# Bit-linear stage: the largest value of each token found hidden block by hidden block on TensorE, four blocks rounded on GpSimd, and the experts' semaphores cleared one stage later

## The reference, cut to what matters

```python
def act_quant(x):
    scale = 127.0 / jnp.clip(jnp.max(jnp.abs(x), axis=-1, keepdims=True), 1e-05)
    return jnp.clip(jnp.round(x * scale), -128, 127) / scale

def bit_linear(x, w):
    xq = x + jax.lax.stop_gradient(act_quant(x) - x)
    wq = w + jax.lax.stop_gradient(weight_quant(w) - w)
    return jnp.einsum('bsd,hd->bsh', xq, wq)

h = bit_linear(x, w1)                                    # 256 -> 1024
h = depthwise_conv1d(h.transpose(0, 2, 1), conv_w, conv_b)   # 3 taps along the tokens
h = h.transpose(0, 2, 1)
h = jax.nn.silu(h)
return bit_linear(h, w2)                                 # 1024 -> 256
```

## Time and profile before

| | us |
|---|---|
| median of 3 runs | 638.29 |
| lowest and highest | 637.61, 638.93 |
| the profiled execution, its own time | 635.03 |
| its span (first to last instruction) | 633.3 |

### The profile page before, as it was taken

How to read it: one execution, slowest core, us unless ns; L and a number is a source line. 1 busy time by engine, 2 the same in 40 slices (tenths; PEclk the granted TensorE clock), 3 DMA queues, 4 the chain that set the end, 5 groups by cost and what they waited for, 6 DMA issues and landing times. The chain is left out here.

```text
span 633.3 us, 14611 instructions
## 1 busy us (share of the span) xinstructions
PE 538.1 (85%) x5264; PEld 460.8 (73%) x5264; DVE 366.0 (58%) x1114; ACT 361.5 (57%) x859; POOL 194.2 (31%) x285
## 2 busy tenths in 40 slices
PE   3899999999977249999999996688999999977565
PEld 2777778888765149999999996667878888756344
DVE  3667666757664811131223103589778877866986
ACT  2678778878764003333222333378788787865544
POOL 2032535335314251111122002621333544424071
PEclk9989999999999559999999998899999999997778
DMA  6472012110201996766755523320201110000001
GB/s 164 141 201 80 27 50 75 52 50 8 73 2 31 331 374 193 278 178 210 258 167 173 166 79 87 110 85 9 93 2 51 51 51 2 3 2 1 1 0 59
DMA packets 33529, 62.79 MB, mean 99 GB/s; under 512 B 4162, under 2 KB 24467, under 8 KB 33332
## 3 DMA queue, kind: packets, MB, share of 16 engines
q1 hardware_dynamic: 29716, 47.97, 23.5%
q0 software_dynamic: 2928, 10.75, 5.8%
q10 hardware_dynamic: 816, 3.15, 1.3%
HBM read 51.11 MB, written 10.75 MB: 98 GB/s over the span
## 5 line engine op out<-in xcount | busy, mean ns | idle before, releaser
L1576 ACT ACTIVATE ex_h_t<-ex_h,b_e 128x128 f32<-128x128 f32 x168 | 48.0, 368 | 125.7 <-PE ex_h L1760 125.7
L1166 PEld LDWEIGHTS a_ring<-ident,w_all 112*125 112x125 f32 x768 | 88.7, 188 | 23.7 <-issue 12.7
L1166 PE MATMUL a_ring<-ident,w_all 112*125 112x112 f32 x768 | 100.1, 280 | 6.4 <-ACT w_all L626 6.3
L634 ACT ACTIVATE w_all<-a_ring 125x448 f32<-125x448 f32 x128 | 62.8, 542 | 45.0 <-PE a_ring L1166 45.0
L1760 PE MATMUL ex_h<-ex_xg_t,w_s 128*128 128x128 f32 x672 | 80.2, 279 | 0.3 <-issue 0.3
L1760 PEld LDWEIGHTS ex_h<-ex_xg_t,w_s 128*128 128x128 f32 x672 | 78.5, 195 | 0.5 <-issue 0.5
L869 DVE TENSOR_REDUCE a_mx<-a_s 112x2 f32<-112x750 f32 x64 | 59.6, 931 | 30.4 <-PE a_s L1157 30.4
L1779 PE MATMUL ex_y<-w_all,ex_h_t 128*128 x336 | 75.9, 379 | 0.0
L876 DVE CUSTOM_DVE_ANT_0 w_all<-a_s,mask_sb 112x375 f32<-112x375 f32 x128 | 65.4, 544 | 16.5 <-PE a_ring L36 10.9
L626 ACT ACTIVATE w_all<-w_all,a_shift 112x375 f32<-112x375 f32 x128 | 69.7, 601 | 6.6 <-DVE a_shift L881 4.8
L1682 DVE TENSOR_TENSOR ex_y_sb<-ex_y,b_all 128x256 f32<-128x256 f32 x21 | 8.9, 425 | 104.9 <-PE ex_y L1779 104.7
(11 more groups left out here) (304 smaller groups left out, 818.0 us busy)
## 6 DMA issues: line engine op xcount, KB each, us to landing
w_s<-in_L_ffn_W SPq DMA_DIRECT2D x18, 1024.0 KB, 5.5
w_all<-in_L_ffn_W SPq DMA_DIRECT2D x8, 1024.0 KB, 11.7
ct_dram<-a_ct SPq DMA_DIRECT2D x8, 752.0 KB, 4.4
a_ct<-ct_dram POOLq DMA_DIRECT2D x8, 752.0 KB
w_s<-in_L_ffn_W ACTq DMA_DIRECT2D x3, 1024.0 KB, 10.9
w_all<-in_ctx SPq DMA_DIRECT2D x8, 375.0 KB
y_slots<-ex_y_sb SPq DMA_DIRECT2D x21, 128.0 KB, 1.7
w_ud<-in_L_ffn_w SPq DMA_DIRECT2D x2, 1024.0 KB, 9.4
```

The lines of the kernel that those rows point to most:

```text
L634: a.activation(et[:, t % 2, kc], bank("et", t, kc)[0:KP, 0:4 * S], ACT.Copy)\
L1166: last = nc.tensor.transpose(bank("et", t, kc)[0:KP, r * S:(r + 1) * S], es[:, t % 2, r, kc * KP:(kc + 1) * KP], ident[0:S, 0:S])
L1576: last = a.activation(h_t[:, i % 2, f], hb[i % 2][:, f * 128:(f + 1) * 128], ACT.Gelu, bias=b1_e[:, i % 2, f:f + 1])
```

## The change

Three things change in the bit-linear stage, and one at the starts of stages.

1. The partial maxima over blocks (`top_of`, `bf_top`) go. Instead each unit's `bf_hs` is turned by TensorE as it is (four transposes a unit, `highest(half, j)`), and VectorE reduces each turned unit with absolute values into `peak`, which now has eight columns. Both are put into the loops over `j`: TensorE does `up(half, j)` and then `highest(half, j - 2)`, VectorE does `taps(half, j)` and then `highest(half, j - 2)`. TensorE's `highest` waits for `silu` of its unit, and from the third unit on for VectorE's reduction of the unit two before, as there are two banks `bf_a`.
2. GpSimd rounds four blocks of half 0 instead of five. `token_scale(0)` stands ahead of half 1's taps, and so `diagonal(0)`, `spread(0)` and `spread_copied` move up. `down_first(0)` and `down_first(1)` stand between the last `up` of half 1, and `turned` one unit later.
3. `begin_phase(first)` of stage a1 clears nothing; the experts' semaphores are cleared with a1's at the start of the bit-linear stage, in one instruction.

The whole diff, without the lines that only declare the semaphore `top_out`:

```diff
@@ -56,12 +56,12 @@
         phase_sems.append(nc.alloc_semaphore(name))
         return phase_sems[-1]
 
-    def begin_phase():
-
-
-        if past_sems:
+    def begin_phase(clear=True):
+
+
+        if past_sems and clear:
             nc.clear_and_free_semaphores(list(past_sems))
-        past_sems.clear()
+            past_sems.clear()
         past_sems.extend(phase_sems)
         phase_sems.clear()
 
@@ -344,7 +344,7 @@
                 def by_row_group(t, e):
                     return t.rearrange("p (n r e d) -> p n r e d", r=4, e=2, d=DH)[:, :, :, e]
 
-                begin_phase()
+                begin_phase(first)
                 with nc.Block(no_gpsimd_drain=True) as block:
                     @block.sync
                     def _(sp):
@@ -1806,8 +1806,7 @@
                 hs = sb("bf_hs", [128, FC, T])
                 hr = sb("bf_hr", [128, 4, HALF], I32)
                 hq = sb("bf_hq", [128, FC, T], BF16)
-                top = sb("bf_top", [128, 2, HALF])
-                peak = sb("bf_peak", [S, B, 2])
+                peak = sb("bf_peak", [S, B, FC])
                 spread_0 = sb("bf_spread_0", [128, HALF])
                 gp = sb("bf_gp", [128, 2, HALF])
                 nought = sb("bf_nought", [128, S], BF16)
@@ -1859,7 +1857,7 @@
                     return slice(half * HALF, (half + 1) * HALF)
 
 
-                GR = 5
+                GR = 4
 
                 def nth(half, j):
                     return FC * half + j - GR
@@ -1942,15 +1940,15 @@
                         for half in range(2):
                             middle(half, 0)
                             middle(half, 1)
+                            if half:
+                                diagonal(0)
                             for j in range(FC):
                                 if j + 2 < FC:
                                     middle(half, j + 2)
                                 if half == 0 and j == 5:
                                     upper()
                                 silu(half, j)
-                                if half and j == 1:
-                                    diagonal(0)
-                                if half and j == 2:
+                                if half and j == 0:
                                     spread_copied()
                         diagonal(1)
                         for j in range(GR, FC):
@@ -1994,21 +1992,16 @@
                             v.scalar_tensor_tensor(conv[:, n % 3, :, 0:S - 1], u[:, :, 1:S], cw[:, j, 2:3],
                                                    conv[:, n % 3, :, 0:S - 1], ALU.mult, ALU.add).then_inc(c_right, 1)
 
-                        def top_of(half, part, first, end):
-
-                            dve.wait_ge(s_out, FC * half + end)
-                            v.tensor_reduce(top[:, part], hs[:, first:end, columns(half)].rearrange("p j t -> p t j"), AX.X, ALU.max,
-                                            apply_absolute_value=True).then_inc(top_out, 1)
-
-                        def highest(half, part):
-                            dve.wait_ge(a_ps, half + part + 1)
-                            v.tensor_reduce(peak[:, HB * half:HB * half + HB, part], pa[part][0:S, :].rearrange("p (b f) -> p b f", b=HB),
-                                            AX.X, ALU.max).then_inc(m_out, 1)
+                        def highest(half, j):
+                            n = FC * half + j
+                            dve.wait_ge(a_ps, n + 1)
+                            v.tensor_reduce(peak[:, HB * half:HB * half + HB, j], pa[n % 2][0:S, :].rearrange("p (b f) -> p b f", b=HB),
+                                            AX.X, ALU.max, apply_absolute_value=True).then_inc(m_out, 1)
 
                         def token_scale(half):
-                            dve.wait_ge(m_out, 2 * half + 1)
+                            dve.wait_ge(m_out, FC * half + FC)
                             bs = slice(HB * half, HB * half + HB)
-                            scales(1, bs, peak[:, bs, 0:half + 1], 1).then_inc(a_out, 1)
+                            scales(1, bs, peak[:, bs], 1).then_inc(a_out, 1)
 
                         def rounded(half, j):
                             m = nth(half, j)
@@ -2030,17 +2023,18 @@
                             taps(0, j)
                             if j == 1:
                                 last_scales()
+                            if j >= 2:
+                                highest(0, j - 2)
                         lower()
-                        top_of(0, 0, 0, FC)
+                        for j in range(FC - 2, FC):
+                            highest(0, j)
+                        token_scale(0)
                         for j in range(FC):
                             taps(1, j)
-                            if j == 0:
-                                highest(0, 0)
-                                token_scale(0)
-                        top_of(1, 0, 0, FC - 2)
-                        top_of(1, 1, FC - 2, FC)
-                        highest(1, 0)
-                        highest(1, 1)
+                            if j >= 2:
+                                highest(1, j - 2)
+                        for j in range(FC - 2, FC):
+                            highest(1, j)
                         token_scale(1)
                         for j in range(GR, FC):
                             rounded(0, j)
@@ -2072,18 +2066,20 @@
                                                             stop=k + part == 2)
                             last.then_inc(u_ps, 1)
 
-                        def highest(half, part):
-                            pe.wait_ge(top_out, half + part + 1)
-                            if half and part == 0:
-                                pe.wait_ge(m_out, 1)
-                            for i in range(HB):
-                                last = nc.tensor.transpose(pa[part][0:S, i * 128:(i + 1) * 128], top[:, part, i * S:(i + 1) * S], ident[:])
+                        def highest(half, j):
+                            n = FC * half + j
+                            pe.wait_ge(s_out, n + 1)
+                            if n >= 2:
+                                pe.wait_ge(m_out, n - 1)
+                            for i, b in enumerate(batches(half)):
+                                last = nc.tensor.transpose(pa[n % 2][0:S, i * 128:(i + 1) * 128], hs[:, j, b * S:(b + 1) * S],
+                                                           ident[:])
                             last.then_inc(a_ps, 1)
 
                         def spread(half):
                             pe.wait_ge(dg, half + 1)
                             if half:
-                                pe.wait_ge(m_out, 3)
+                                pe.wait_ge(m_out, 2 * FC)
                             nc.tensor.matmul(pr[half][:, 0:HALF], ones[0:S, :],
                                              diag[:, HB * half:HB * half + HB].rearrange("p b s -> p (b s)"),
                                              start=True, stop=True).then_inc(r_ps, 1)
@@ -2117,22 +2113,25 @@
 
                         for j in range(FC):
                             up(0, j)
-                            if j == 5:
+                            if j == 6:
                                 turned()
+                            if j >= 2:
+                                highest(0, j - 2)
+                        for j in range(FC - 2, FC):
+                            highest(0, j)
                         for j in range(FC):
                             up(1, j)
                             if j == 2:
-                                highest(0, 0)
-                            if j == 4:
                                 spread(0)
-                        down_first(0)
-                        down_first(1)
-                        highest(1, 0)
-                        down_first(2)
-                        highest(1, 1)
-                        down_first(3)
+                            if j >= 2:
+                                highest(1, j - 2)
+                            if j >= 6:
+                                down_first(j - 6)
+                        for j in range(FC - 2, FC):
+                            highest(1, j)
+                            down_first(j - FC + 4)
                         spread(1)
-                        for j in range(4, FC):
+                        for j in range(GR, FC):
                             down_first(j)
                         for j in range(FC):
                             down_last(j)
```

More of the change, by code:

```diff
@@ L1843, in bit_ffn_phase @@
                 hr_out = sem("bf_hr_out")
-                top_out = sem("bf_top_out")
                 spread_out = sem("bf_spread_out")
```

## The result

The changed kernel takes 643.76 us (median of 6 runs, 641.54 to 646.11) and the kernel before, in the same comparison, 637.36 us (6 runs, 633.41 to 638.93). The ratio is 1.0112, 95% interval 1.0072 to 1.0152: **slower by 1.1%**, 6.4 us by the medians and 7.1 us by the ratio. The prediction said 642.0 us, 639.3 to 647.0.

The account below looks back on a forecast made before the run. VectorE was taken to set the bit-linear stage's pace before, the TensorE-ScalarE loop after. Stage +4.2 us (+4.7 to half 1's scales, -0.5 tail) and clears -0.5 made +3.7 us on 638.29: 642.0 us, range 639.3 to 647.0.

Parts of the forecast that it names:

- The loop: Bit-linear halves: matmuls, `middle`, `silu`, transposes follow one another between TensorE and ScalarE; one turn 2.88 us a unit, 4.02 at low clock.
- The clock: TensorE's clock level in the loop's turns, taken as high; each turn costs 1.14 us more at the low level.
- the rival with the low clock: Clock falls within the bit-linear loop; four of nine turns low add 4.6 us, giving 646.6 us; chance 0.22.
- one of the signs that the prediction named for being wrong: The bit-linear stage's granted clock in the loops being 0.50 would show the forecast wrong.
- The tail: End of bit-linear stage: diagonal and spread 2.6 us, then VectorE's roundings and additions 7.5 us, where before 8.0.
- The half microsecond that should come back: Bit-linear tail: 0.5 us gained, VectorE's roundings and additions taking 7.5 us instead of 8.0 with waits for TensorE.
- The clears: Start of a1: no semaphore clears ahead of GpSimd's first loads, assumed gain 0.5 us, bounds 0 and 0.95.
- the block: Bit-linear tail: VectorE takes a fourth rounding from GpSimd, 0.53 us within the wait for the second spread, costing nothing.
- the prediction's point of decision: Bit-linear loop: VectorE binds at 1.91 us a turn if TensorE could start unit j+1 ahead of the waiting transposes.
- the 632.5 worked out: Rival that VectorE binds: stage gains 4.1 us and 1.2 us of waits, clears 0.5; 632.5 us, chance 0.07.
- No change from shorter turns: Rival: bit-linear turns shorter than rows from a standing start say; 2.47 us each cancels the loss; 638.8 us, chance 0.09.

Follow-up runs that it names:

- experiment 1: Changed kernel with a unit's transposes and reduction three units behind its matmuls instead of two, on TensorE and VectorE: 632.7 us, ratio 0.9923 to the kernel before.
- experiment 3: Changed kernel with `silu(j)` ahead of `middle(j + 2)` on ScalarE, TensorE's and VectorE's order kept: 630.45 us, ratio 0.9881 to the kernel before.
- experiment 2: Kernel before with one TensorE wait exchanged: matmuls of unit n wait for `silu` of unit n - 3, not the bank's last taps: 649.01 us, ratio 1.0159.
- experiments 5 and 6: The profiles meant: changed kernel with three extra TensorE matmuls a unit in half 0, behind units 2 to 7 (637.49 us) and 4 to 7 only (638.35 us).
- The repeat in experiment 5: The changed kernel run again with nothing altered: 643.7 us, ratio 1.01 to the kernel before.
- the first kernel of experiment 6: Changed kernel with three extra TensorE matmuls behind those of units 2 and 3 of half 0 only: 643.55 us, ratio 1.0115 to the kernel before.

## Why the prediction was right

**The loop: right, and its length too.** The trace shows what the prediction named: ScalarE idle ahead of `middle`, ended by TensorE, and TensorE idle 1.28 us ahead of each group of transposes, ended by `silu` (forecast 1.3). A turn is 2.74 us against 2.88 forecast, and 3.87 against 4.02 at the low clock. The 0.14 us are mostly the transposes: their start to the start of the matmuls is 612.37 - 611.97 = 0.40 us and 586.03 - 585.28 = 0.75, where I had counted 0.50 and 0.86. Experiments 1 and 3, which cut the loop at two different places, both give VectorE's 1.90 us a unit, and experiment 2, which has only the loop, has the loss. VectorE's idle time was 0.75 us a unit in half 1 and 1.56 + 0.23 in half 0, for the 0.9 and more of the forecast.

**The clock: the term that was mis-sized.** The step that failed is "I take it as high, but the idle 1.3 us of each turn could tip it". I had taken the level from the rows of 580 to 590 before, where TensorE had begun the stage with 6.83 us of matmuls without a pause; in the changed kernel the first pause comes after 4.82 us, while the clock is still low (0.50 to 580). TensorE's first rows of the stage, before and after:

```profile
574.45 6.83 PE L2070 MATMUL bf_u<-bf_xh,wu_t 128*128 128x448 f32 x20 [1.25 <-PEq L348]
```

```profile
575.31 4.82 PE L2064 MATMUL bf_u<-bf_xh,wu_t 128*128 128x448 f32 x12 [1.25 <-PEq L348]
```

Half 0 had four turns, from 580.16 to 595.66, at 3.87 us. Against 2.88 that is 4.0 us; the last turn adds 0.6, since its transposes (1.10 us for 0.65) and part of its matmuls (1.40 us for 1.08) ran low as well: 30.5 against 25.9 us. Half 1 ran its turns at the high clock and came out 1.2 us shorter than forecast (628.04 - 605.83 = 22.2 us against 23.4). Half 0 is 4.6 us over the forecast, half 1 1.2 us under it and the tail 0.6 us over: the 4.0 us by which the stage was mis-sized. So the rival with the low clock, put at 0.22 with just four such turns, described the profiled execution better than the forecast did: 59.4 + 4.6 = 64.0 us of stage for 63.4 measured. And one of the signs that the prediction named for being wrong came, a granted clock of 0.50 in a loop, in half 0. The two are one mechanism, and how many turns are slow differs from run to run.

That the time came within 1.8 us of the forecast is in part luck. The change was put at +3.7 us and measured at 6.4 by the medians, and the kernel before was 0.9 us quicker in the comparison than the 638.29 us that the forecast started from. Within the stage two errors had opposite signs: the two profiles with high turns throughout (experiments 5 and 6) took 56.8 and 56.6 us where the forecast, with high turns, had 59.4, and low turns made it 63.4. The Trainium skill (TensorE: Matmul & The Clock Gate, section "A second HAM failure mode: psum-queue depth-cycling") speaks of a clock that goes back and forth when TensorE idles briefly between groups. The prediction held that the trace agreed only for longer idling. The repeat in experiment 5 and the first kernel of experiment 6 agree with the page, the clock having fallen after pauses of 1.28 us; half 1 of the changed kernel, with five of them at the high level, doesn't show it.

**The tail: nearly.** Roundings and additions took 638.73 - 631.25 = 7.5 us, as forecast. From the end of the scales to the first of them it was 3.2 us and not 2.6, as the second spread ran at the low clock (1.86 us for two matmuls, 1.30 before). The half microsecond that should come back was spent there.

**The clears and the block: right as far as seen.** 0.54 us at GpSimd for an assumed 0.5; its way to the end stays open. The moved block costs and gains nothing that could be measured.

**The rivals that fell.** VectorE doesn't bind in the changed kernel, but the prediction's point of decision was right: where the order lets TensorE go on, it is 632.7 us (experiment 1) for the 632.5 worked out. That the totals meet so closely is chance in part: its stage gained 3.7 us where the rival counted 5.3, and experiment 3, which lets VectorE bind as well, gained 6.4. No change from shorter turns would have needed 2.47 us.

## What to carry to other kernels

When a step is put into an in-order engine's program, follow the ring that it closes: which engine's work it waits for, what stands ahead of that there, and whether that again waits for this engine. The sum around the ring, not any engine's busy time, is the pace; here 2.7 to 3.9 us against 1.9. Such a ring is cut by one unit more of distance, or by the order of two calls on the other engine, and that turned a loss of 1.1% into a gain of 0.8% by the first and 1.2% by the second. Look also at the clock in the rows of a loop in which TensorE pauses each turn, and in the rows just ahead of it, before taking either level.

## What was not expected of the hardware

The same loop, with TensorE idle for 1.28 us in each turn at either level, was seen at 1.00 and at 0.50 of the clock, and went from one to the other inside one half in two kernels; a turn costs 1.13 us more at the low level. Adding work in the pauses, 0.77 us of it per turn, made the kernel 7.5 us faster than leaving TensorE idle. What decides in which turn the clock falls isn't settled: filling the opening alone changed nothing (1.0115 against 1.0112), and five pauses in a row left it high in half 1. Clearing two ranges with 35 semaphores together took GpSimd 0.54 us.
